# The last norm of a graph network: PE transposes only, DVE adds the residual, and the last sum takes 16 tiles for each group

## The chip, the cores and the metric

The kernel runs on one core of a Trainium2 chip. The metric is device time in microseconds (us) of one execution; lower is better.

## The reference

Four graph layers over 3,125 nodes with 96 features and 100,000 edges, each preceded by a row normalisation and a ReLU and added to the node features. The change touches what lies between the end of the third and the fourth, cut here to:

```python
# end of layer 2 (h comes from its second attention convolution)
h = _graph_norm(h, gn_weight, gn_bias, gn_mean_scale)   # per feature: scale, shift
x = x + _leaky(h + residual, 0.01)
# before layer 3
h = jnp.maximum(_layernorm(x, axis=-1), 0.0)            # per node
# layer 3
norm = deg_inv_sqrt[row] * deg_inv_sqrt[col]
x = x + segment_sum(h[col] * norm[:, None], row)
```

`_leaky(v, s)` is v where v >= 0, else s * v.

## The kernel before

The nodes lie in 25 tiles of 128 rows (NT = 25), taken in 5 groups of 5 tiles (G = 5, NG = 5). The sum over edges is a product with a dense adjacency of 3,200 x 3,200 counts in fp16 (`k.ADJ`), in 25 x 25 blocks of 128 x 128. The summand is split in a high and a low fp16 half (`k.Y`, 192 columns), so a block is one matmul of 128 x 192.

`graph_norm` makes a scale and a shift per feature from column statistics. `last_norm` then runs on all engines at once, each with its own written order and semaphores between them:

- The convolution's output stands turned (features on partitions) in PSUM. ACT, `scaled(g)`, L1964: scale and shift of a group into SBUF (`turned[g]`).
- PE, `raise_rows(g)`: the residual `R` goes through an identity matmul in fp32 into the group's bank (L2008), and five matmuls with an identity turn the scaled tiles back and add them (L2011). `raised(g)` is bank 4 + g % 4.
- Leaky ReLU in two parts, since v + leak = 0.99 relu(v) + 0.01 v. ACT, `bent(g)`, L1971: 0.99 relu of the bank into R. DVE, `bend(g)`, L1897: x + that; `add(g)`, L1901: + 0.01 of the bank.
- DVE, `statistics` (L1909), `moments` (L1914, and the variance, L673), `scales` (L1919 to L1923); ACT, the root (L688), then `rows(g)`: the five tiles normalised with ReLU (L1976) and the high half (L1979). DVE, `low(g)`, L1928: the low half, after which Y of the group is ready.
- PE, L2019: 625 products. `sums(j)` are half banks, tiles 0 to 7 in banks 0 to 3, tiles 8 to 15 in banks 4 to 7, later tiles again from bank 0. `over_chunk(m, first, end)` adds Y's group m to the tiles first to end. Before: groups 0 to 3 for 8 tiles (AT_ONCE = 8), then, after `added` of all groups (the banks of the raise are free), groups 0 to 3 for the next 8, group 4 for all 16, then tiles 16 to 24 one by one.
- DVE, at last, adds the halves (L1954) and the result to x (L1949); SP stores.

ACT's written order is scaled 0 to 3, bent 0, scaled 4, bent 1, bent 2, and for each group the root, bent of g + 3, rows. DVE's order is a loop over g with the six functions staggered. PE first runs 28 matmuls that feed nothing (FILL = 28, L1999).

SP: `load_back` (L1391) loads the residual and the kept x from memory, 5 loads of 240 KB each, in turn (L1394, L1395); behind them on the same queue are the last 6 of 25 transposed loads of the adjacency (L1401), which the products of the last two groups need.

Of the kernel before, what the change touches and what calls it, by code (L numbers as in the profile page):

```python
# [14 lines left out]
ALU = mybir.AluOpType  # L15
ACT = mybir.ActivationFunctionType
# [110 lines left out]
def flat(ap):  # L127
    return ap.rearrange("p a b -> p (a b)")
# [1262 lines left out]
def load_back(k, d, sp):  # L1391

    for g in range(NG):
        sp.dma_start(tiles(k.R, g), tiles(d.residual, g)).then_inc(k.r_back, 16)  # L1394
        sp.dma_start(tiles(k.X, g), tiles(d.kept_x, g)).then_inc(k.x_back, 16)  # L1395


# [467 lines left out]


LEAK = 0.01
FILL = 28


def last_norm(nc, k, d, c, block):

    s = semaphores(nc, k, "last", "scaled raised bent rest added measured row_moments variance deviation row_scale row_factor row_shift "
                   "normal high y_ready unscaled summed emptied final stored")
    R = k.R
    held = flat(k.H[:, :, :])
# [12 lines left out]

    @block.vector
    def _(dve):
        def bend(g):
            dve.wait_ge(s.bent, g + 1)
            dve.wait_ge(k.x_back, 16 * NG)
            dve.tensor_tensor(tiles(k.X, g), tiles(k.X, g), tiles(R, g), ALU.add).then_inc(s.rest, 1)  # L1897

        def add(g):
            dve.wait_ge(s.rest, g + 1)  # L1900
            nc.vector.scalar_tensor_tensor(out=flat(tiles(k.X, g)), in0=raised(g), scalar=LEAK, in1=flat(tiles(k.X, g)),  # L1901
                                           op0=ALU.mult, op1=ALU.add).then_inc(s.added, 1)

        def statistics(g):
            dve.wait_ge(s.added, g + 1)
# [22 lines left out]
            nc.vector.scalar_tensor_tensor(out=part(k.Y, 1, g), in0=tiles(R, g), scalar=SCALE, in1=part(k.Y, 0, g), op0=ALU.mult,  # L1928
                                           op1=ALU.subtract).then_inc(s.y_ready, 1)

        for g in range(NG + 2):
            if g < NG:
                bend(g)
            if 1 <= g <= NG:
                statistics(g - 1)
            if g < NG:
                add(g)
            if 1 <= g <= NG:
                moments(g - 1)
            if g >= 2:  # L1940
                low(g - 2)
            if 1 <= g <= NG:
                scales(g - 1)
        dve.tensor_scalar(k.inv_deg[:, :], k.dis[:, :], 1 / (SCALE * UNIT), None, ALU.mult).then_inc(s.unscaled, 1)
        dve.wait_ge(s.unscaled, 1)

# [13 lines left out]
    @block.scalar  # L1960
    def _(act):
        def scaled(g):
            for t, a, z in turned_spans(g * G, (g + 1) * G):
                last = nc.scalar.activation(turned[g][:, (t - g * G) * P:(t - g * G) * P + z - a], flat(k.ps[0:C, :, :])[:, a:z],  # L1964
                                            ACT.Identity, scale=k.scale, bias=k.shift)
            last.then_inc(s.scaled, 1)

        def bent(g):

            act.wait_ge(s.raised, g + 1)  # L1970
            nc.scalar.activation(flat(tiles(R, g)), raised(g), ACT.Relu, scale=1 - LEAK).then_inc(s.bent, 1)  # L1971

        def rows(g):
            act.wait_ge(s.row_shift, g + 1)
            for t in range(g * G, (g + 1) * G):
                nc.scalar.activation(R[:, t, :], k.X[:, t, :], ACT.Relu, scale=k.row_scale[:, t:t + 1],  # L1976
                                     bias=k.row_shift[:, t:t + 1]).then_inc(s.normal, 1)
            act.wait_ge(s.normal, G * (g + 1))
            nc.scalar.activation(part(k.Y, 0, g), tiles(R, g), ACT.Copy, scale=SCALE).then_inc(s.high, 1)  # L1979

        act.wait_ge(k.affine, 1)
        for g in range(4):
            scaled(g)
        bent(0)
        scaled(4)
        bent(1)
        bent(2)
        for g in range(NG):
            act_row_deviation(nc, k, act, s, g)
            if g + 3 < NG:  # L1990
                bent(g + 3)
            rows(g)

    @block.tensor
    def _(pe):
        def keep_busy(times):

            for _ in range(times):
                nc.tensor.matmul(raised(0)[:, 0:P], k.ident_h[:, :], k.ident_h[:, :], start=True, stop=True)  # L1999

        def raise_rows(g):

            if g >= 4:
                pe.wait_ge(s.added, g - 3)
            elif g >= 1:
                pe.wait_ge(s.scaled, g)
            pe.wait_ge(k.r_back, 16 * NG)
            nc.tensor.matmul(raised(g), k.ident[:, :], flat(tiles(R, g)), start=True, stop=False)  # L2008
            pe.wait_ge(s.scaled, g + 1)
            for t in range(G):  # L2010
                last = nc.tensor.matmul(raised(g)[:, t * C:(t + 1) * C], turned[g][:, t * P:(t + 1) * P], k.ident[0:C, 0:C],  # L2011
                                        start=False, stop=t == G - 1)
            last.then_inc(s.raised, 1)

        def product(j, i):
# [12 lines left out]
                if m == NG - 1 and j % 2:  # L2028
                    last.then_inc(s.summed, 1)

        keep_busy(FILL)
        for g in range(NG):
            raise_rows(g)
        for m in range(NG - 1):
            over_chunk(m, 0, AT_ONCE)
        pe.wait_ge(s.added, NG)
        for m in range(NG - 1):
            over_chunk(m, AT_ONCE, 2 * AT_ONCE)
        over_chunk(NG - 1, 0, 2 * AT_ONCE)
        for j in range(2 * AT_ONCE, NT):  # L2040

            if j % 2 == 0:
# [129 lines left out]
```

## Time and profile before

| | us |
|---|---|
| median of 3 timed executions | 868.24 |
| their lowest and highest | 868.05, 868.81 |
| the profiled execution, all in all | 876.73 |
| its span (all times of the trace run from its start) | 875.0 |
| PE, DVE, ACT busy in it | 750.4, 626.6, 481.2 |
| last stage, from PE's fill to the span's end | 794.3 to 875.0 |

The trace gives for every instruction its start and length; "idle before" is how long its engine had nothing, and what ended that. A PE length includes the way through the array, so lengths of neighbours overlap, and the pace is read from starts. The fp32 matmul has two entries for each instruction. "PEclk" or granted clock is 1.00 at 2.4 GHz and 0.50 at 1.2 GHz.

### The profile page before, as it was taken

The page shows a single profiled execution, that of the slowest core. Times are in us where ns is not written, and L with a number is a line of the kernel's source. Part 1 is how long each engine was busy: PE and PEld are TensorE (multiplying, and loading weights), DVE is VectorE, ACT ScalarE, POOL GpSimd, SP SyncE. Part 2 cuts the span into 40 slices and gives each one's busy share as a digit, 9 for nine tenths or more (in the row PEclk, how much of TensorE's full clock was granted, in tenths as well). Part 3 has the DMA queues.
Part 4 walks back from the last instruction along what each step waited for, and adds up shares of the span by engine and source line. Part 5 has one row for each costly group of instructions (what it writes and reads, how often), then busy time and mean ns, then how long its engine had stood idle before and what let it go on. Part 6 is the DMA issues. An engine that isn't in the chain of part 4 may idle for free. (4 is left out here: it accounts for less than half of the span.)

```text
span 875.0 us, 21046 instructions
## 1 busy us (share of the span) xinstructions
PE 750.4 (86%) x8192; PEld 677.5 (77%) x8192; DVE 626.6 (72%) x1691; ACT 481.2 (55%) x916; POOL 4.3 (0%) x14
## 2 busy tenths in 40 slices
PE   7888888868988999999997399988656999887898
PEld 6655556548987998999997298887655898776797
DVE  7899999985355454433444789998787999885632
ACT  2798889861004222212235578887576988773600
POOL 1000000000000000000000000000000000000000
PEclk9799999998997999999997589999956999996999
DMA  4000000007960000000002100000000699839401
GB/s 135 11 12 12 12 3 1 1 5 262 413 282 1 2 1 2 2 1 1 13 24 81 33 16 4 16 17 1 1 14 20 141 176 200 169 80 233 106 22 36
DMA packets 98739, 56.06 MB, mean 64 GB/s; under 512 B 91160, under 2 KB 93130, under 8 KB 98504
## 3 DMA queue, kind: packets, MB, share of 16 engines
q1 hardware_dynamic: 98292, 53.78, 22.3%
q8 instruction: 69, 1.13, 0.5%
q10 hardware_dynamic: 340, 0.84, 0.3%
q14 instruction: 38, 0.31, 0.1%
HBM read 9.16 MB, written 24.97 MB: 39 GB/s over the span
## 5 line engine op out<-in xcount | busy, mean ns | idle before, releaser
L614 PE MATMUL banks<-y_sb,adjacency 128*128 128x192 f16 (+1 forms) x1875 | 166.4, 249 | 8.5 <-DVE y_sb L651 7.8
L614 PEld LDWEIGHTS banks<-y_sb,adjacency 128*128 128x128 f16 x1875 | 162.0, 99 | 9.5 <-DVE y_sb L651 7.9
L457 PE MATMUL counts<-hot_code,hot_row 128*128 128x100 f16 (+3 forms) x1568 | 122.3, 217 | 23.2 <-DVE hot_code L351 17.6
L457 PEld LDWEIGHTS counts<-hot_code,hot_row 128*128 128x128 f16 x1568 | 90.7, 99 | 66.0 <-DVE hot_code L351 41.3
L1752 PE MATMUL banks<-loose,y_sb 128*128 128x194 f16 x540 | 101.1, 251 | 0.0
L1751 PE MATMUL banks<-x_sb,gat_masks 128*128 128x194 f16 x420 | 79.6, 251 | 20.7 <-DVE gat_masks L1676 6.8
L351 DVE TENSOR_TENSOR hot_code<-codes_iota,unpacked 128x600 f16<-128x600 f16 x196 | 96.7, 552 | 0.0
L560 ACT ACTIVATE adjacency<-counts 128x800 f16<-128x800 f32 x98 | 81.7, 834 | 21.5 <-PE counts L457 21.4
L1751 PE MATMUL banks<-x_sb,y_sb 128*128 128x194 f16 x400 | 75.1, 250 | 13.6 <-DVE h_sb L1676 9.9
L1724 ACT ACTIVATE gat_masks<-y_sb,node_scalars 128x640 bf16<-128x640 f32 x84 | 68.0, 825 | 26.5 <-PE banks L1752 19.3
L1751 PE MATMUL banks<-x_sb,h_sb 128*128 128x194 f16 x430 | 75.8, 247 | 0.8
L1085 ACT ACTIVATE y_sb<-banks 96x256 f32<-96x256 f32 x50 | 19.1, 382 | 97.2 <-PE banks L1117 97.2
L344 DVE TENSOR_TENSOR hot_row<-rows_iota,unpacked 128x2560 f16<-128x2560 f16 x49 | 72.4, 1478 | 0.0
L1752 PE MATMUL banks<-loose,h_sb 128*128 128x194 f16 x400 | 72.4, 247 | 0.0
L1724 ACT ACTIVATE y_sb<-y_sb,node_scalars 128x640 bf16<-128x640 f32 x80 | 64.9, 825 | 10.6 <-PE banks L1752 9.7
L1724 ACT ACTIVATE h_sb<-y_sb,node_scalars 128x640 bf16<-128x640 f32 x86 | 68.2, 825 | 0.4
L640 DVE TENSOR_REDUCE y_sb<-banks 128x96 f32<-128x192 f32 x50 | 17.9, 357 | 65.8 <-PE banks L614 65.8
L539 ACT ACTIVATE distance<-codes_iota,negative 128x100 f16<-128x100 f16 x196 | 57.4, 367 | 11.6 <-DVE negative L336 11.6
L1751 PEld LDWEIGHTS banks<-x_sb,gat_masks 128*128 128x128 f16 x420 | 41.7, 99 | 26.4 <-DVE y_sb L1670 13.1
L640 DVE TENSOR_REDUCE h_sb<-banks 128x96 f32<-128x192 f32 x50 | 17.8, 356 | 59.3 <-PE banks L614 58.8
L1752 PE MATMUL banks<-loose,gat_masks 128*128 128x194 f16 x310 | 58.9, 250 | 0.0
L614 PE MATMUL banks<-loose,adjacency 128*128 128x192 f16 x625 | 55.9, 248 | 0.0
(246 smaller groups left out, 1358.4 us busy)
## 6 DMA issues: line engine op xcount, KB each, us to landing
kept_adj<-adjacency SPq DMA_DIRECT2D x5, 4000.0 KB, 31.8
y_sb<-a_dst_rows SPq DMA_DIRECT2D x10, 320.0 KB, 3.4
window_keys<-edge_keys SPq DMA_DIRECT2D x188, 5.0 KB
residual<-h_sb SPq DMA_DIRECT2D x5, 240.0 KB, 2.0
kept_x<-x_sb SPq DMA_DIRECT2D x1, 1200.0 KB, 4.6
loose<-residual SPq DMA_DIRECT2D x5, 240.0 KB, 4.6
x_sb<-kept_x SPq DMA_DIRECT2D x5, 240.0 KB, 4.8
x_sb<-in_x SPq DMA_DIRECT2D x4, 240.0 KB
```

Source lines behind the costliest of these rows:

```text
L344: dve.tensor_tensor(hot_row[:, h, :, :].rearrange("p n (a b) -> p n a b", b=2), rows_iota[:, :].rearrange("p (a b) -> p a b", b=2).unsquee ...
L351: dve.tensor_tensor(hot_codes(h, b).rearrange("p w (a b) -> p w a b", b=2), codes_iota[:, FROM[b]:FROM[b] + WIDE[b]].rearrange("p (a b) -> ...
L457: last = nc.tensor.matmul(counts[:, 2 * (p % HELD) + i, start:end], hot_row[:, q % 2, b * QUAD + w, :], hot_codes(q % 2, b)[:, w, start - ...
L539: nc.scalar.activation(distance[:, q % 2, w, :], codes_iota[:, FROM[-1]:CODES], ACT.Abs, bias=negative[:, load % 2, at:at + 1]).then_inc(d ...
L560: nc.scalar.activation(k.ADJ[:, :, 2 * p * W:2 * (p + 1) * W].rearrange("p t (b o) -> p t b o", o=W), counts_of(2 * (p % HELD), 2), ACT.Co ...
L614: return nc.tensor.matmul(k.ps[:, j % G, 0:cols], k.ADJ[:, i, j * P:(j + 1) * P], y[:, i, 0:cols], start=i == 0, stop=i == NT - 1)
L640: return nc.vector.tensor_reduce(out, k.ps[:, b, 0:ONE].rearrange("p (q f) -> p f q", q=PARTS), axis=AX, op=ALU.add)
L1085: nc.scalar.activation(HT[:, j % 2, :], k.ps[0:C, TURNED, 0:2 * P], ACT.Copy).then_inc(v.copied, 1)
L1724: nc.scalar.activation(step_of(x), row[ch % 2], ACT.Relu, bias=k.a_s5[:, i:i + 1], scale=STEEP).then_inc(t.step_ready, 1)
L1751: nc.tensor.matmul(bank[:, 0:2 * BC], over_of(x)[:, q * P:(q + 1) * P], features[0][:, i, :], start=i == 0, stop=False)
L1752: return nc.tensor.matmul(bank[:, 2 * BC:4 * BC], under_of(x)[:, q * P:(q + 1) * P], features[1][:, i, :], start=False, stop=i == NT - 1)
```

## The change

- `load_back` issues the five residual loads first and then the five of kept x.
- PE's `raise_rows` only transposes; the identity matmul of R and PE's wait for the residual are gone. The waits on `scaled` stay; for group 4 it waits for the first `lifted`.
- DVE: `lift(g)` adds the residual to the bank, into R; `bend(g)` is max(0.01 R, R) in place; `add(g)` adds it to x. ACT's `bent` is gone.
- DVE's and ACT's written orders are new.
- PE's fill is 32 instead of 28, and a second one of 48 stands behind the raise, into bank 0.
- The sum takes 8 tiles for group 0, waits for all five `lifted`, takes the next 8 for group 0, and then 16 tiles for each of the groups 1 to 4. Tiles 16 to 24 are as before.

```diff
     for g in range(NG):
         sp.dma_start(tiles(k.R, g), tiles(d.residual, g)).then_inc(k.r_back, 16)
+    for g in range(NG):
         sp.dma_start(tiles(k.X, g), tiles(d.kept_x, g)).then_inc(k.x_back, 16)
...
-FILL = 28
+FILL, FILL_MORE = 32, 48
...
+        def lift(g):
+            dve.wait_ge(s.raised, g + 1)
+            dve.wait_ge(k.r_back, 16 * NG)
+            dve.tensor_tensor(flat(tiles(R, g)), raised(g), flat(tiles(R, g)), ALU.add).then_inc(s.lifted, 1)
+
         def bend(g):
+            dve.wait_ge(s.lifted, g + 1)
+            nc.vector.scalar_tensor_tensor(out=tiles(R, g), in0=tiles(R, g), scalar=LEAK, in1=tiles(R, g),
+                                           op0=ALU.mult, op1=ALU.max).then_inc(s.bent, 1)
+
+        def add(g):
             dve.wait_ge(s.bent, g + 1)
             dve.wait_ge(k.x_back, 16 * NG)
-            dve.tensor_tensor(tiles(k.X, g), tiles(k.X, g), tiles(R, g), ALU.add).then_inc(s.rest, 1)
-
-        def add(g):
-            dve.wait_ge(s.rest, g + 1)
-            nc.vector.scalar_tensor_tensor(out=flat(tiles(k.X, g)), in0=raised(g), scalar=LEAK, in1=flat(tiles(k.X, g)),
-                                           op0=ALU.mult, op1=ALU.add).then_inc(s.added, 1)
+            dve.tensor_tensor(tiles(k.X, g), tiles(k.X, g), tiles(R, g), ALU.add).then_inc(s.added, 1)
...
-        for g in range(4):
+        for g in range(NG):
             scaled(g)
-        bent(0)
-        scaled(4)
-        bent(1)
-        bent(2)
         for g in range(NG):
             act_row_deviation(nc, k, act, s, g)
-            if g + 3 < NG:
-                bent(g + 3)
             rows(g)
...
             if g >= 4:
-                pe.wait_ge(s.added, g - 3)
-            elif g >= 1:
-                pe.wait_ge(s.scaled, g)
-            pe.wait_ge(k.r_back, 16 * NG)
-            nc.tensor.matmul(raised(g), k.ident[:, :], flat(tiles(R, g)), start=True, stop=False)
+                pe.wait_ge(s.lifted, g - 3)
             pe.wait_ge(s.scaled, g + 1)
             for t in range(G):
-                last = nc.tensor.matmul(raised(g)[:, t * C:(t + 1) * C], turned[g][:, t * P:(t + 1) * P], k.ident[0:C, 0:C],
-                                        start=False, stop=t == G - 1)
+                last = nc.tensor.transpose(raised(g)[:, t * C:(t + 1) * C], turned[g][:, t * P:(t + 1) * P], k.ident[0:C, 0:C])
             last.then_inc(s.raised, 1)
...
-        keep_busy(FILL)
+        keep_busy(raised(0)[:, 0:P], FILL)
         for g in range(NG):
             raise_rows(g)
-        for m in range(NG - 1):
-            over_chunk(m, 0, AT_ONCE)
-        pe.wait_ge(s.added, NG)
-        for m in range(NG - 1):
-            over_chunk(m, AT_ONCE, 2 * AT_ONCE)
-        over_chunk(NG - 1, 0, 2 * AT_ONCE)
+        keep_busy(sums(0)[:, 0:P], FILL_MORE)
+        over_chunk(0, 0, AT_ONCE)
+        pe.wait_ge(s.lifted, NG)
+        over_chunk(0, AT_ONCE, 2 * AT_ONCE)
+        for m in range(1, NG):
+            over_chunk(m, 0, 2 * AT_ONCE)
```

DVE's written order, where `last_norm` begins. Names of tiles: `loose` holds R, `x_sb` holds x, `banks` is PSUM, `mean` the row deviations. Before:

```order
L1897 TENSOR_TENSOR x_sb<-x_sb,loose 128x480
L1901 SCALAR_TENSOR_TENSOR x_sb<-banks,x_sb 128x480
L1897 TENSOR_TENSOR x_sb<-x_sb,loose 128x480
L1909 BN_STATS y_sb<-x_sb 128x6 x5
L1901 SCALAR_TENSOR_TENSOR x_sb<-banks,x_sb 128x480
L1914 BN_AGGR node_scalars<-y_sb 128x2 x5
L673 TENSOR_SCALAR mean<-node_scalars 128x5
L1919 RECIPROCAL mean<-mean 128x5
```

The same place now:

```order
L1898 TENSOR_TENSOR loose<-banks,loose 128x480
L1902 SCALAR_TENSOR_TENSOR loose<-loose 128x480
L1898 TENSOR_TENSOR loose<-banks,loose 128x480
L1908 TENSOR_TENSOR x_sb<-x_sb,loose 128x480
L1902 SCALAR_TENSOR_TENSOR loose<-loose 128x480
L1915 BN_STATS y_sb<-x_sb 128x6 x5
L1908 TENSOR_TENSOR x_sb<-x_sb,loose 128x480
L1920 BN_AGGR node_scalars<-y_sb 128x2 x5
L673 TENSOR_SCALAR mean<-node_scalars 128x5
L1898 TENSOR_TENSOR loose<-banks,loose 128x480
L1925 RECIPROCAL mean<-mean 128x5
```

Five operations of 128x480 stand before the first statistics instead of three, and a lift of group 2 stands between the first variance and its reciprocal.

DVE further on, from the first scales to the first low half (L1934), now:

```order
L1929 SCALAR_TENSOR_TENSOR node_scalars<-node_scalars 128x5
L1902 SCALAR_TENSOR_TENSOR loose<-loose 128x480
L1915 BN_STATS y_sb<-x_sb 128x6 x5
L1908 TENSOR_TENSOR x_sb<-x_sb,loose 128x480
L1920 BN_AGGR node_scalars<-y_sb 128x2 x5
L673 TENSOR_SCALAR mean<-node_scalars 128x5
L1898 TENSOR_TENSOR loose<-banks,loose 128x480
L1934 SCALAR_TENSOR_TENSOR y_sb<-loose,y_sb 128x5x96
```

Before, the same piece was L1923, L1897, L1909, L1901, L1914, L673, L1928: the bend and the add were there too, and the lift of group 3 is new in it.

PE's written order, from the first fill to the products. Before:

```order
L1999 MATMUL banks<-ident_h 128x128 x28
L2008 MATMUL banks<-loose,ident 128x480
L2011 MATMUL banks<-ident,h_sb 128x96 x5
L2008 MATMUL banks<-loose,ident 128x480
L2011 MATMUL banks<-ident,h_sb 128x96 x5
```

Now:

```order
L1999 MATMUL banks<-ident_h 128x128 x32
L2007 MATMUL banks<-ident,h_sb 128x96 x15
L2007 MATMUL banks<-ident,y_sb 128x96 x10
L1999 MATMUL banks<-ident_h 128x128 x48
L2014 MATMUL banks<-y_sb,adjacency 128x192 x625
```

The matmuls out of `loose` are gone, and the second fill stands directly ahead of the 625 products.

## Rows read from the trace of the kernel before

**Rows 1.** The page of the profile, its first line
```profile
span 875.0 us, 21046 instructions
```

**Rows 2.** The chain that ended last, its last 83 us (start us, length us, engine, tile, line)
```profile
798.08 1.97 PE banks L2008 x2
800.04 2.08 PE banks L2011 x10
...
813.30 0.57 ACT loose L1971
...
816.32 0.66 DVE y_sb L1928
...
828.40 42.34 PE banks L2019 x505
870.76 0.36 DVE h_sb L1954
```

**Rows 3.** PE in order of time in the last stage (start us, length us)
```profile
794.32 3.15 PE L1999 MATMUL banks<-ident_h 128*128 128x128 f16 x28 [2.23 <-PEq L1414]
...
813.10 1.00 PE L2008 MATMUL banks<-loose,ident 128*128 128x480 f32 x2
813.93 1.25 PE L2011 MATMUL banks<-ident,y_sb 96*128 96x96 f32 x10
817.13 3.50 PE L2019 MATMUL banks<-y_sb,adjacency 128*128 128x192 f16 x40 [1.94 <-DVE y_sb L1928]
820.88 3.50 PE L2019 MATMUL banks<-y_sb,adjacency 128*128 128x192 f16 x40 [0.26 <-DVE y_sb L1928]
```

**Rows 4.** Four stretches: PE's busy time, granted clock, DMA share, GB/s
```profile
264.00:270.50 6.50, 5.02 (x25) 0.50 0.00 0
504.30:513.00 8.70, 8.66 (x76) 0.71 0.01 2
792.60:813.00 20.40, 18.07 (x76) 0.50 1.10 254
813.10:817.00 3.90, 2.08 (x14) 1.00 1.12 250
```

**Rows 5.** ACT in order of time, last stage
```profile
796.64 2.67 ACT L1964 ACTIVATE h_sb<-banks,node_scalars 96x640 f32<-96x640 f32 x4 [0.67 <-DVE node_scalars L1857]
...
813.77 1.89 ACT L1976 ACTIVATE loose<-x_sb,node_scalars 128x96 f32<-128x96 f32 x5
815.69 0.60 ACT L1979 ACTIVATE y_sb<-loose 128x480 f16<-128x480 f32 x1
```

**Rows 6.** DVE in order of time, last stage
```profile
802.76 0.66 DVE L1897 TENSOR_TENSOR x_sb<-x_sb,loose 128x480 f32<-128x480 f32 x1 [6.16 <-ACT loose L1971]
803.46 0.66 DVE L1901 SCALAR_TENSOR_TENSOR x_sb<-banks,x_sb 128x480 f32<-128x480 f32 x1
...
810.75 0.17 DVE L1923 SCALAR_TENSOR_TENSOR node_scalars<-node_scalars 128x5 f32<-128x5 f32 x1
810.83 0.66 DVE L1897 TENSOR_TENSOR x_sb<-x_sb,loose 128x480 f32<-128x480 f32 x1
811.40 0.89 DVE L1909 BATCH_NORM_STATS2 y_sb<-x_sb 128x6 f32<-128x96 f32 x5
812.21 0.64 DVE L1901 SCALAR_TENSOR_TENSOR x_sb<-banks,x_sb 128x480 f32<-128x480 f32 x1
812.77 0.43 DVE L1914 BATCH_NORM_AGGREGATE node_scalars<-y_sb 128x2 f32<-128x6 f32 x5
```

**Rows 7.** PE in order of time in an earlier stage: transposes of the same shape
```profile
264.38 2.93 PE L954 MATMUL banks<-ident,loose 96*128 96x96 f32 x15 [3.52 <-ACT loose L910]
...
268.86 1.06 PE L954 MATMUL banks<-ident,loose 96*128 96x96 f32 x5 [0.20 <-ACT loose L910]
```

**Rows 8.** SP's queue in order of time: last load of kept x, transposed loads
```profile
793.15 0.43 SPq L1395 DMA_DIRECT2D x_sb<-kept_x  x1
794.27 22.87 SPq L1401 DMA_TRANSPOSE adjacency<-kept_adj  x6
```

More of the change, by code:

```diff
@@ L1867 @@
 LEAK = 0.01
-FILL = 28
+FILL, FILL_MORE = 32, 48
 def last_norm(nc, k, d, c, block):
-    s = semaphores(nc, k, "last", "scaled raised bent rest added measured row_moments variance deviation row_scale row_factor row_shift "
+    s = semaphores(nc, k, "last", "scaled raised lifted bent added measured row_moments variance deviation row_scale row_factor row_shift "
                    "normal high y_ready unscaled summed emptied final stored")
@@ L1929, in low @@
                                            op1=ALU.subtract).then_inc(s.y_ready, 1)
[L1931 to L1943, printed above, removed]
+        lift(0)
+        bend(0)
+        lift(1)
+        add(0)
+        bend(1)
+        for g in range(NG):
+            statistics(g)
+            if g + 1 < NG:
+                add(g + 1)
+            moments(g)
+            if g + 2 < NG:
+                lift(g + 2)
+            if g >= 1:
+                low(g - 1)
+            scales(g)
+            if g + 2 < NG:
+                bend(g + 2)
+        low(NG - 1)
         dve.tensor_scalar(k.inv_deg[:, :], k.dis[:, :], 1 / (SCALE * UNIT), None, ALU.mult).then_inc(s.unscaled, 1)
@@ L1966, in scaled @@
             last.then_inc(s.scaled, 1)
-        def bent(g):
-            act.wait_ge(s.raised, g + 1)
-            nc.scalar.activation(flat(tiles(R, g)), raised(g), ACT.Relu, scale=1 - LEAK).then_inc(s.bent, 1)
         def rows(g):
@@ L1981, in _ @@
         act.wait_ge(k.affine, 1)
-        for g in range(4):
+        for g in range(NG):
             scaled(g)
-        bent(0)
-        scaled(4)
-        bent(1)
-        bent(2)
         for g in range(NG):
             act_row_deviation(nc, k, act, s, g)
-            if g + 3 < NG:
-                bent(g + 3)
             rows(g)
@@ L1995, in _, with keep_busy @@
     def _(pe):
-        def keep_busy(times):
+        def keep_busy(at, times):
             for _ in range(times):
-                nc.tensor.matmul(raised(0)[:, 0:P], k.ident_h[:, :], k.ident_h[:, :], start=True, stop=True)
+                nc.tensor.matmul(at, k.ident_h[:, :], k.ident_h[:, :], start=True, stop=True)
         def raise_rows(g):
             if g >= 4:
-                pe.wait_ge(s.added, g - 3)
-            elif g >= 1:
-                pe.wait_ge(s.scaled, g)
-            pe.wait_ge(k.r_back, 16 * NG)
-            nc.tensor.matmul(raised(g), k.ident[:, :], flat(tiles(R, g)), start=True, stop=False)
+                pe.wait_ge(s.lifted, g - 3)
             pe.wait_ge(s.scaled, g + 1)
             for t in range(G):
-                last = nc.tensor.matmul(raised(g)[:, t * C:(t + 1) * C], turned[g][:, t * P:(t + 1) * P], k.ident[0:C, 0:C],
-                                        start=False, stop=t == G - 1)
+                last = nc.tensor.transpose(raised(g)[:, t * C:(t + 1) * C], turned[g][:, t * P:(t + 1) * P], k.ident[0:C, 0:C])
             last.then_inc(s.raised, 1)
```

## The prediction

> **What bounds the kernel now.** I begin with the span [rows 1]: 875.0 us. The profiled execution took 876.73 us in all, 1.7 us more than its span; the three timed executions have a median of 868.24 us, 8.5 us less. The sum below is made against the profiled execution and then carried to the median.
>
> Next comes the chain that ended last, over its last 83 us [rows 2]. It runs through PE (from 798.08, when the residual is there: one identity matmul and five half-matmuls for each group of rows, four groups until 813.30), ACT (bend of group 3, then the rows of group 0), DVE (low half of group 0), and then the sum, whose last 505 matmuls run without a gap from 828.40 to 870.74. So the stage has two halves: a run-up that ends when the first group of Y is ready, and 625 matmuls at 42.34 / 505 = 0.0838 us each, 52.4 us that nothing shortens. The question is when the first of them can start and how much PE waits among them.
>
> PE's own order of time [rows 3] answers both. The first product starts at 817.13. The next group's start is 820.88, 3.75 us later, but 40 products take only 3.35 us, so PE waits 0.40 us in each of three gaps, 1.2 us in all. The granted clock [rows 4] is 0.50 (1.2 GHz) from 792.6 to 813.0, while PE was busy for 18.07 of 20.4 us, and 1.00 (2.4 GHz) after that.
>
> ACT [rows 5] shows why the run-up is so long. It is strictly in order: its rows of group 0 start at 813.77, after the bend of group 3 that waited for PE until 813.30. DVE [rows 6] had the row shift of group 0 ready at 810.92. So 2.9 us are lost to ACT's queue, and the rest to PE, which needs 3.8 us a group (15.22 us for four) at the low clock.
>
> **What the change removes.** For each group the identity matmul of 128x480 in fp32 goes (1.7 us: the 3.8 less the 2.08 below) and the half-matmuls, 2.08 us for five [rows 2], become transposes. The same shape, 96x96 in fp32 out of 96x128 weights, is in the trace as transposes at the same 0.50 clock: five in 1.06 us [rows 7], and 15 in 2.93 us, so 0.9 us a group ((2.93 - 1.06) / 2) when they follow one another. ACT loses its five bends, 0.57 us each, and with them its waits for PE. PE no longer waits for the residual.
>
> **The new run-up, step by step.**
> 1. PE fills first: 28 matmuls took 3.15 us from 794.32 [rows 3], 0.1125 us each, so 32 end at 797.92. ACT's first scaled group, at most 0.9 us from 796.64 (three groups, one of them in two pieces, take 2.67 [rows 5]), is done at 797.5 and so hidden. Group 0 is raised at 797.92 + 1.06 = 798.98, group 1 at 799.9, and with 0.9 us a group the last at 802.5. ACT's scaling (0.8 us a group, the last done at about 800.9) hides behind that.
> 2. DVE's lift is an add of 128x480 with one operand in PSUM. There is no such row for this operation; the nearest are 0.66 and 0.64 us for the fused op out of PSUM and 0.66 for the add in SBUF [rows 6]. I take the step between starts: 0.57 us where the next doesn't depend on it (810.83 to 811.40), 0.70 where it does (802.76 to 803.46). The price could be 0.5 to 0.9, which moves the run-up by -0.3 to +1.3 us, as four lifts lie in it.
> 3. Lift 0 at 799.04; bend 0 at 799.74; lift 1 at 800.31; add 0 at 800.88; bend 1 at 801.45; five statistics of group 0 at 802.02 (0.81); add 1 at 802.83; five moments at 803.40 (0.47, 0.43 and the handover); variance at 803.87; lift 2 at 803.97, which hides the root on ACT, as small as DVE's own ops on 5 columns (0.17 us and a handover); three scale ops from 804.54 (0.20 each, 0.17 and the handover). Row shift ready at about 805.1.
> 4. ACT: five rows 1.92 us and the high half 0.60 [rows 5], to 807.7.
> 5. DVE meanwhile: bend 2, statistics 1, add 2, moments 1, variance and lift 3, 0.57 + 0.81 + 0.57 + 0.47 + 0.10 + 0.57 = 3.09 us from 805.03, so low 0 starts at 808.1, not at 807.7: DVE is the last to come. It takes 0.66, and 0.15 us later PE starts, as before. **First product 808.9 instead of 817.13: 8.2 us earlier.**
>
> **What is hidden.** The second fill: 48 matmuls from 802.5 at 0.1125 us are 5.4 us, to 807.9, 1.0 us before Y comes. If the raise were later than I have it, this fill would delay the first product one for one. The loads [rows 8]: the five residual loads are issued first, with no load of kept x between them, and so land before the 798.08 at which PE had them; lift 0 wants them at 799.0. Kept x keeps its last issue at 793.15, and add 0 wants it 7.7 us later. The six transposed loads of the adjacency behind them keep their place on SP's queue; they are issued by 817.1, and the last group's products start at 808.9 + 4 x 6.7 = 835.7. DVE's group costs 4.4 us (0.57 more lift than before, 0.6 of it no longer hidden behind ACT), where the period was 3.75.
>
> **The sum over groups.** With 16 tiles a group PE needs 80 x 0.0838 = 6.7 us for each, more than the 4.4 us in which DVE makes one, so the three waits of 0.40 go. One new wait comes: tiles 8 to 15 use the banks of the raise, and PE waits for the fifth lift. It is behind low 0, the scales, bend 3, statistics 2, add 3 and moments 2 on DVE: 808.1 + 0.57 + 0.6 + 0.57 + 0.81 + 0.57 + 0.57 = 811.8, plus 0.66 = 812.4. PE's first 40 products end at 812.3. A wait of 0.1 to 0.2 us. Net -1.0 us.
>
> From the last products on nothing changes: final tiles at 0.49 us each, the last reduce at 870.76 [rows 2], 4.2 us to the span's end. **Sum: -8.2 - 1.0 = -9.2 us**, 867.5 us for the profiled execution, 859.0 from the median. The terms I could not read (lift, root beside a lift, start-up of the transposes) mostly err to the late side, and a clock that is low for part of the first products costs a little; I take 0.8 us for these and forecast **859.8 us**.
>
> **A rule against the change.** The trace first: 25 transposes in 6.5 us left the clock at 0.50 [rows 4], and PE was busy 5.0 us of it. The identity matmuls that go are, on the other hand, the very work after which it rose at 813. The Trainium skill, TensorE: Matmul & The Clock Gate, Part 4 (PE-mode transpose), says that work in transpose mode does not count as PE being busy, so that the full clock does not come from it. By that rule the raise stays at 1.2 GHz and only the fills can lift the clock; the sum above already has the transposes at their 1.2 GHz price, and the rule bears on rival B.
>
> **Rivals.**
> A. *The profiled execution was unlucky in its clock.* Its stage ran 20 us at half clock, and the timed executions were 8.5 us shorter. At full clock a group took 2.08 us (the last, 813.10 to 815.18 [rows 3]). Had the clock been full from the second group on, group 1 would be raised at 801.9 + 2.1 = 804.0, not 805.7, and group 3 at 808.1. The row shift of group 0 came 5.2 us after the raise of group 1, so it would be there at 809.1, and ACT would start its rows then, 4.7 us sooner than at 813.77. The first product would be at 812.4, and the change would bring 3.5 + 1.0 = 4.5 us: 863.7 us. For: 8.5 us have to be somewhere. Against: the three times lie within 0.76 us of each other, which a clock that rises by chance would not give.
> B. *PE starts the sum at 1.2 GHz.* In an earlier stage fp16 products ran densely from 504.3 on, and the mean clock over the 8.7 us from there is 0.71 [rows 4]: 5 us at 0.50 and 3.7 at 1.00. If the second fill's 5.4 us don't lift it, or it falls in the pause before Y, the first 3.5 to 5.5 us of products run at twice the time, a loss of 1.7 to 2.8 us: 860.7 to 861.8 from the sum's 859.0. For: a clock of 0.50 all through the first fill. Against: the second fill is 5.4 us of fp16 matmuls, and there the clock rose 5 us after such work began, and it did not fall in the pause of 1.94 us before 817.13 [rows 3, 4]. (The skill's rule above speaks for B as well.)
> C. *DVE is slower in the run-up than the sum has it.* It has one more pass over each group. If PSUM reads cost 0.9 us and each handover to a dependent op 0.1 us more, 2 to 3 us of the 9 go: 861 to 862.
> D. *Slower than before.* The clock stays low through the sum's first part as it did through the raise: 20.4 us at 0.50 though PE was busy 18.07 of them. From 808.9 on, each us at 1.2 GHz costs half a us, so the change turns into a loss when the low stretch is over 18.5 us; at 20.4 us it costs 10.2 and gives 869.2 us. Against: the products of 504.3 had the full clock after 5 us.
> E. *The change doesn't do what it says*: PE stalls on the fifth lift for long, because DVE's queue places it behind three groups' work. It would need DVE to be late by more than the 3.35 us of cover; each us late is a us lost. I see 0.1 to 0.2.
>
> **How the numbers follow.** Forecast with its small terms 0.56 (858 to 861), A 0.18 (862 to 865), B 0.14, C 0.08, D 0.03, E 0.01. About 0.2%, 1.7 us, is what a measurement of this kernel can tell from no change, so faster means under 866.5. Only the far end of A, and D, are not: faster 0.93, same 0.03, slower 0.04. The range, 857.3 to 865.0, takes in the sum without allowance and the cheap end of the lift (-0.3), a fill that finds the clock high (1 to 1.4 us), and the whole of B and C and most of A.
>
> **What would show it.** In the profile after: no idle PE before the first transposes, five of them in about 1.06 us at clock 0.50; ACT's rows of group 0 at 10.8 us after PE's first fill begins (805.1 - 794.32; it was 19.5); the first product at 14.6 us after it (808.9 - 794.32; it was 22.8); no idle PE before the second to fifth groups but for the wait on the lift, under 0.3 us; clock 1.00 at the first product. Wrong: a first product over 16 us after the fill begins (C, or the fill itself in its way), the clock at 0.50 there (B, D), or a profile that shows 9 us gained where the times show 5 (A).

## The result and the profile after

| | before | changed |
|---|---|---|
| median of 22 executions each, lowest to highest (us) | 874.0 (868.05 to 878.0) | 868.61 (865.23 to 870.04) |
| profiled execution, its span | 876.73, 875.0 | 869.12, 867.3 |
| PE's first fill begins (in the trace) | 794.32 | 794.89 |
| first product, after the fill's start | 22.81 | 14.22 |
| 625 products, first to last | 53.59 | 53.97 |

The ratio to the kernel before is 0.9946, 95% interval 0.9929 to 0.9964: about 4.7 us faster (3.1 to 6.2), or 5.4 us between the medians. The forecast was 8.4 us. The time itself, 868.61 us, lies above the range that ended at 865.0. Times between kernels are compared below from PE's first fill on, since that point lies at 792.2 to 795.0 us in these traces for reasons ahead of the change, and the place of that point goes into every execution's time.

The page's first line after the change:

```profile
span 867.3 us, 21079 instructions
```

The chain that ended last (start, length, engine, tile, line), which answers [rows 2]:

```profile
794.89 3.57 PE banks L1999 x32
798.46 2.12 PE banks L2007 x15
800.58 0.63 DVE loose L1898
...
804.18 0.66 DVE loose L1898
...
805.82 0.89 DVE y_sb L1915 x5
...
808.40 0.58 DVE y_sb L1934
...
809.11 53.98 PE banks L2014 x625
...
863.12 0.36 DVE h_sb L1965
```

The run-up no longer goes through ACT. From the first raised groups (line 2007) it is DVE all the way to the low half of group 0 (line 1934, 808.40), and the sum is one piece of 625.

PE in order of time, against [rows 3]:

```profile
794.89 3.57 PE L1999 MATMUL banks<-ident_h 128*128 128x128 f16 x32 [2.31 <-PEq L1415]
798.25 2.31 PE L2007 MATMUL banks<-ident,h_sb 96*128 96x96 f32 x15
...
802.01 2.85 PE L1999 MATMUL banks<-ident_h 128*128 128x128 f16 x48
809.11 53.97 PE L2014 MATMUL banks<-y_sb,adjacency 128*128 128x192 f16 x625 [4.25 <-DVE y_sb L1934]
```

Fifteen transposes, three groups, take 2.31 us where the old raise took 3.8 us for each group. The second fill is over at 804.86, PE has nothing for 4.25 us, and the first product comes at 809.11.

The granted clock, against [rows 4] (stretch, length, PE's busy time and count, clock, DMA share, GB/s):

```profile
792.90:799.70 6.80, 4.81 (x42) 0.50 1.10 283
799.90:810.00 10.10, 5.47 (x75) 1.00 1.09 237
810.10:813.40 3.30, 3.30 (x24) 0.50 1.10 248
813.50:817.00 3.50, 3.50 (x44) 1.00 1.36 227
```

The clock rose at 799.8, among the transposes of the raise, was full for all of the second fill, fell at 810.0, 0.9 us after the first product, and was full again at 813.4. So 3.4 us of products ran at half speed, and 53.97 is 1.6 us more than 625 x 0.0838 = 52.4.

ACT and DVE in order of time, against [rows 5, 6]:

```profile
805.37 1.90 ACT L1982 ACTIVATE loose<-x_sb,node_scalars 128x96 f32<-128x96 f32 x5 [0.86 <-DVE node_scalars L1929]
807.30 0.60 ACT L1985 ACTIVATE y_sb<-loose 128x480 f16<-128x480 f32 x1
```

```profile
799.29 0.66 DVE L1898 TENSOR_TENSOR loose<-banks,loose 128x480 f32<-128x480 f32 x1 [2.12 <-PE banks L2007]
799.99 0.66 DVE L1902 SCALAR_TENSOR_TENSOR loose<-loose 128x480 f32<-128x480 f32 x1
800.56 0.65 DVE L1898 TENSOR_TENSOR loose<-banks,loose 128x480 f32<-128x480 f32 x1
...
804.18 0.66 DVE L1898 TENSOR_TENSOR loose<-banks,loose 128x480 f32<-128x480 f32 x1
...
807.74 0.66 DVE L1898 TENSOR_TENSOR loose<-banks,loose 128x480 f32<-128x480 f32 x1
808.32 0.65 DVE L1934 SCALAR_TENSOR_TENSOR y_sb<-loose,y_sb 128x480 f16<-128x480 f32 x1
```

Step by step from the fill's start (794.89), measured and in brackets forecast: lift 0 at 4.40 (4.72), bend 0 at 5.10 (5.42), lift 2 at 9.29 (9.65), ACT's rows at 10.48 (10.8), low 0 at 13.43 (13.8), first product 14.22 (14.6). The lift takes 0.66 us, or 0.57 to the next start, like the operation in SBUF. The new run-up is what the prediction said, 0.3 to 0.4 us early throughout. The clock isn't the reason: lift 0 started at 799.29, before the clock rose, and was already 0.32 us early. The sum let the first transposes start when the fill was over, 3.60 us after it began; they started 3.36 us after it (798.25), as the records of neighbours overlap. The faster transposes after that gained nothing, since lift 1 came 0.57 us after bend 0, at DVE's own pace.

### The profile page after: what moved, and what is told of

Its sections match the earlier page's. It is cut to its first block and busy times, and to the rows that moved or that the text cites. A ratio compares the mean times of both kernels' runs of the same rounds, so it can differ in the third digit from the quotient of the medians.

```text
span 867.3 us, 21079 instructions
## 1 busy us (share of the span) xinstructions
PE 740.7 (85%) x8209; PEld 670.8 (77%) x8209; DVE 629.3 (73%) x1696; ACT 478.6 (55%) x911; POOL 4.3 (0%) x14
## 3 DMA queue, kind: packets, MB, share of 16 engines
q1 hardware_dynamic: 98292, 53.78, 22.8%
## 5 line engine op out<-in xcount | busy, mean ns | idle before, releaser
L2014 PE MATMUL banks<-y_sb,adjacency 128*128 128x192 f16 x625 | 54.0, 250 | 4.3 <-DVE y_sb L1934 4.3
```

Source lines behind the costliest of these rows:

```text
L2014: return nc.tensor.matmul(sums(j), k.ADJ[:, a * G + i % G, at:at + P], k.Y[:, i, 0:ONE], start=i == 0 and j % 2 == 0, stop=i == NT - 1 and ...
```

## Experiments

Four sets were run, each on one chip together with the kernel before, whose median in the set stands beside (870.88, 875.59, 874.79, 874.65). The last two columns are from the one trace that each has.

| run | median us (n) | before in its set | ratio, 95% interval | first product after fill | products |
|---|---|---|---|---|---|
| changed, again | 867.61 (12) | 870.88 | 0.9942, 0.9919 to 0.9965 | 14.22 | 53.97 |
| old order of products | 867.62 (12) | 870.88 | 0.9953, 0.9928 to 0.9978 | 14.23 | 53.97 |
| bridge, 80 fills | 865.73 (7) | 870.88 | 0.9924, 0.9894 to 0.9954 | 14.22 | 52.48 |
| no second fill | 868.96 (12) | 870.88 | 0.9956, 0.9930 to 0.9982 | 14.22 | 54.44 |
| before, again | 875.14 (12) | 875.59 | 1.0011, 0.9977 to 1.0045 | 16.10 | 53.60 |
| before, new order alone | 876.87 (12) | 875.59 | 1.0023, 0.9989 to 1.0056 | 22.96 | 56.70 |
| before, first fill of 60 | 871.03 (12) | 875.59 | 0.9971, 0.9942 to 0.9999 | 17.46 | 53.97 |
| short chain, 80 fills | 865.82 (10) | 875.59 | 0.9909, 0.9879 to 0.9939 | 13.98 | 52.34 |
| short chain, 36 fills | 866.55 (7) | 874.79 | 0.9917, 0.9889 to 0.9946 | 12.84 | 54.84 |
| own chain, 36 fills | 868.89 (12) | 874.79 | 0.9942, 0.9921 to 0.9963 | 14.22 | 54.44 |
| loads in turn | 868.39 (12) | 874.79 | 0.9938, 0.9917 to 0.9959 | 14.22 | 53.97 |
| short chain, 42 fills | 866.26 (6) | 874.65 | 0.9905, 0.9880 to 0.9931 | 12.85 | 52.34 |

The ratio compares all executions of a set and isn't the quotient of the two medians, which swing with the kernel before: its median alone lies anywhere from 870.9 to 875.6 us.

### The kernel before, once more: where its time goes up and down

No edit.

> The kernel before as it is, for more of its own executions with their clocks and one more trace. Theory 1 (the clock in the raise is what makes it vary): executions from 868 to 878 us; where PE's clock rises in the raise, a group takes about 2.1 instead of 3.7 us and the first product comes up to 4.7 us sooner after PE's first fill than the 22.8 us of the trace known so far. Theory 2: the first product is always 22.8 us after the fill, and the variation comes from elsewhere in the program.

Its profiled execution took 870.26 us, and its trace differs from the first one in the raise. PE in order of time:

```profile
794.53 3.15 PE L1999 MATMUL banks<-ident_h 128*128 128x128 f16 x28 [2.08 <-PEq L1414]
798.15 1.76 PE L2008 MATMUL banks<-loose,ident 128*128 128x480 f32 x2 [0.47 <-DMA loose<-residual]
799.75 1.25 PE L2011 MATMUL banks<-ident,h_sb 96*128 96x96 f32 x10
800.83 1.00 PE L2008 MATMUL banks<-loose,ident 128*128 128x480 f32 x2
...
807.44 1.25 PE L2011 MATMUL banks<-ident,y_sb 96*128 96x96 f32 x10
810.63 3.50 PE L2019 MATMUL banks<-y_sb,adjacency 128*128 128x192 f16 x40 [1.94 <-DVE y_sb L1928]
```

The clock in the same trace (the same columns as above):

```profile
792.80:799.50 6.70, 4.50 (x30) 0.50 1.08 283
799.70:810.60 10.90, 8.99 (x59) 1.00 1.11 243
```

And ACT, where its rows of group 0 start:

```profile
807.27 1.89 ACT L1976 ACTIVATE loose<-x_sb,node_scalars 128x96 f32<-128x96 f32 x5
```

Here the clock was full from 799.6 on, a group of the old raise took 1.93 us (798.15 + 2.7 for the first, then 800.83, 802.76), ACT began its rows of group 0 at 807.27 and not at 813.77, and the first product came at 810.63, 16.1 us after the fill began and not 22.8. The span is 868.5 us, 6.5 us shorter than in the first trace; the stage makes 6.7 of it. The 132 executions of the kernel before in all sets fall in two heaps: 47 from 867 to 872 us and 85 from 872 to 880, with 76 of these between 874 and 878. The two traces, 870.26 and 876.73 us, stand one in each. That every execution of the lower heap has the early clock is inferred, not seen in each, but two numbers on record agree with it. Of the 110 executions in the four sets, whose mean granted clock is known, it is 0.933 or more in 21 of the 37 below 872 us and in none of the 73 above. And the heaps have means of 869.5 and 875.6 us, 6.1 us apart, where the stage differs by 6.7. What makes the clock rise early in one execution and late in another was not found. The first three timed executions, on which the prediction stood, were all of the lower heap.

### Only a longer first fill in the kernel before

```diff
-FILL = 28
+FILL = 60
```

> The kernel before with a first fill of 60 matmuls instead of 28. Theory 1: the clock is full at the start of the raise; it starts about 2.3 us later (800.3 for 798.0) but takes 2.1 us a group, so the first product comes 3.5 to 4.5 us sooner than in the known trace, the median falls by 2 to 4 us, and the executions lie within 3 us of each other. Theory 2: the raise starts later and gains nothing, 0 to 3 us slower.

PE in order of time in this kernel, and a stretch of its granted clock:

```profile
794.64 5.88 PE L1999 MATMUL banks<-ident_h 128*128 128x128 f16 x60 [2.17 <-PEq L1414]
...
812.10 53.97 PE L2019 MATMUL banks<-y_sb,adjacency 128*128 128x192 f16 x625 [1.94 <-DVE y_sb L1928]
```

```profile
812.10:816.60 4.50, 4.50 (x36) 0.63 1.22 213
```

The fill took 5.9 us, the clock was full from 799.7, the raise ran at 1.92 us a group, and the first product came 17.46 us after the fill began: 5.3 us sooner than in the first trace, though PE started its raise 2.0 us later after that point. Eleven of twelve executions lie between 869.16 and 872.37 us (one outlier of 1821 us aside), so the upper heap is gone. The median fell by 4.6 us against 875.59 in the set; by the ratio, 0.9971, it is 2.5 us, and the interval, 0.9942 to 0.9999, is wide, since the kernel beside it varies. The clock fell here too, at 813.3, 1.2 us after the first product, and cost the products 1.6 us (53.97). One number in the old kernel thus gave about half of what the whole change gave: 2.5 us of 4.7 by the two ratios, whose intervals overlap. The changed kernel lies 2.2 us lower by the ratios and 3.0 us by the means of its 34 executions and these eleven (867.99 and 870.97); in the traces the two differ by 3.2 us in this stage (17.46 - 14.22).

### The new order of products alone

In the kernel before, PE's `over_chunk` calls replaced by those of the changed kernel, with `added` for `lifted`:

```diff
-        for m in range(NG - 1):
-            over_chunk(m, 0, AT_ONCE)
+        over_chunk(0, 0, AT_ONCE)
         pe.wait_ge(s.added, NG)
-        for m in range(NG - 1):
-            over_chunk(m, AT_ONCE, 2 * AT_ONCE)
-        over_chunk(NG - 1, 0, 2 * AT_ONCE)
+        over_chunk(0, AT_ONCE, 2 * AT_ONCE)
+        for m in range(1, NG):
+            over_chunk(m, 0, 2 * AT_ONCE)
```

> The kernel before with only the new order of products (8 tiles of group 0, a wait for the last add, the next 8, then 16 tiles for each later group). The fifth add of the old run-up ends 6.0 us after the first product starts, 2.7 us after the first 40 products: PE waits 2.7 us once instead of 1.2 us in three gaps. So this part alone should cost 1.5 us; a gain of 1 us would mean that the order is good by itself.

PE waited 2.60 us for the fifth add, as expected, and the products took 56.70 us, 3.1 more than before, where 1.5 were expected: the clock fell as well, at 823.2 when PE resumed, and was low for 3.4 us, which costs another 1.7. Against its neighbours the median is 1.3 to 1.7 us higher; the ratio's interval, 0.9989 to 1.0056, doesn't exclude no change. In the old run-up the new order brings nothing, and no run shows it bringing anything in the new one (below).

### The changed kernel again, and with the old order of products

> The changed kernel as it is, as the measure for its neighbours. Theory 1 (clock): the second fill ends early when the clock is already full, PE then idles some 4 us before the first product, the clock falls, and the first 3 to 4 us of products run at 1.2 GHz: 625 products take about 54.0 us from the first to the last, 1.6 more than at full clock. Theory 2 (run-up or chance): nothing systematic in the clock; a new execution shows the products in 52.4 us. Against the kernel before, 4 to 7 us less by either.

> The changed kernel with the old order of the products (8 tiles for groups 0 to 3, the next 8 tiles afterwards). PE then waits for DVE before groups 1 to 3: starts of the groups 4.13, 3.76 and 3.76 us apart where 40 products take 3.35, 1.6 us of waiting. If my sum is right (the 16 tiles a group bring 1.0 us at full clock) this is 1.0 to 1.4 us slower than the changed kernel. If the clock is low at the first product (theory 1), the slow products fall into those waits, and the difference is 0 to 0.5 us. If 16 tiles a group were the main part of the gain, it would be 3 us or more.

```diff
-        over_chunk(0, 0, AT_ONCE)
-        pe.wait_ge(s.lifted, NG)
-        over_chunk(0, AT_ONCE, 2 * AT_ONCE)
-        for m in range(1, NG):
-            over_chunk(m, 0, 2 * AT_ONCE)
+        for m in range(NG - 1):
+            over_chunk(m, 0, AT_ONCE)
+        pe.wait_ge(s.lifted, NG)
+        for m in range(NG - 1):
+            over_chunk(m, AT_ONCE, 2 * AT_ONCE)
+        over_chunk(NG - 1, 0, 2 * AT_ONCE)
```

The changed kernel repeats to 0.01 us: 14.22 and 53.97. With the old order nothing changes, 867.62 against 867.61 us and again 53.97 us: the 625 products follow one another without a gap in both. At half clock the first of them take longer, which gives DVE the time. The 1.0 us that the prediction gave to this part does not show. What the new order would bring at full clock was not tried.

### The clock at the first product: more fill, none, and where it stands

```diff
-        keep_busy(sums(0)[:, 0:P], FILL_MORE)
+        keep_busy(sums(0)[:, 0:P], 24)
+        pe.wait_ge(s.row_moments, G)
+        keep_busy(sums(0)[:, 0:P], 24)
+        pe.wait_ge(s.row_shift, 1)
+        keep_busy(sums(0)[:, 0:P], 24)
+        pe.wait_ge(s.high, 1)
+        keep_busy(sums(0)[:, 0:P], 8)
```

> The changed kernel with the second fill of 48 matmuls cut in four and spread over the wait for Y: 24 after the raise, 24 after the moments of group 0, 24 after its row shift, 8 after its high half. Theory 1: the clock is full at the first product, the 625 products take 52.4 to 52.6 us, and the kernel is 1.3 to 1.7 us faster than the changed one. Theory 2: no difference (within 0.3 us).

PE in order of time in the kernel with the bridge, from the second fill on:

```profile
799.42 1.50 PE L1999 MATMUL banks<-ident_h 128*128 128x128 f16 x24
801.54 2.85 PE L1999 MATMUL banks<-ident_h 128*128 128x128 f16 x48 [0.62 <-DVE node_scalars L1920]
805.37 0.62 PE L1999 MATMUL banks<-ident_h 128*128 128x128 f16 x8 [0.98 <-ACT y_sb L1985]
806.52 52.48 PE L2014 MATMUL banks<-y_sb,adjacency 128*128 128x192 f16 x625 [0.53 <-DVE y_sb L1934]
```

Its granted clock:

```profile
797.30:806.50 9.20, 6.72 (x96) 1.00 1.13 251
806.50:812.00 5.50, 5.48 (x64) 1.00 1.13 205
```

With PE kept at work until Y is there the clock stays at 1.00 and the products take 52.48 us, 1.49 less. The first product is where it was, 14.22 us after the fill. The median is 1.9 us below the changed kernel's in the same set; all seven executions are under 866.7, though the intervals of the two ratios overlap. Theory 1 stands by the traces.

No second fill at all:

```diff
-FILL, FILL_MORE = 32, 48
+FILL, FILL_MORE = 32, 0
```

> The changed kernel without the second fill. Theory 1: PE idles from the raise to the first product, 6 to 7 us, so the clock is always low there and comes 3.4 to 6 us later: 54.0 to 55.2 us for the products, 0 to 1.2 us slower than the changed kernel, as the fill of 48 already loses most of its purpose. Theory 2: no difference.

PE in order of time in this kernel, and then its granted clock:

```profile
807.60 54.44 PE L2014 MATMUL banks<-y_sb,adjacency 128*128 128x192 f16 x625 [6.93 <-DVE y_sb L1934]
```

```profile
798.50:801.70 3.20, 1.80 (x16) 1.00 1.10 249
801.90:811.90 10.00, 4.30 (x28) 0.50 1.09 235
812.10:816.00 3.90, 3.90 (x49) 1.00 1.11 240
```

PE idles for 6.93 us, the clock is low from 801.8 and full again from 812.0, 4.4 us into the sum, and the products take 54.44 us, 0.47 more than with the fill of 48. The median is 1.35 us higher than the changed kernel's, of which the stage shows 0.47. By the products, the second fill as written gives 0.47 of the 1.96 us (54.44 - 52.48) that one which bridges the pause gives.

The spread fill again, with 36 in place of 80:

```diff
-        keep_busy(sums(0)[:, 0:P], FILL_MORE)
+        keep_busy(sums(0)[:, 0:P], 14)
+        pe.wait_ge(s.row_moments, G)
+        keep_busy(sums(0)[:, 0:P], 10)
+        pe.wait_ge(s.row_shift, 1)
+        keep_busy(sums(0)[:, 0:P], 8)
+        pe.wait_ge(s.high, 1)
+        keep_busy(sums(0)[:, 0:P], 4)
```

> The changed kernel with its own order on DVE and the spread fill of 36 matmuls instead of one fill of 48 (14 after the raise, 10 after the moments, 8 after the row shift, 4 after the high half). If it is the place of the fill and not its amount that keeps the clock, the products take 52.4 to 52.6 us and this is as fast as the bridge of 80, 1.3 to 1.9 us faster than the changed kernel, with 12 matmuls less. If the amount counts, the clock falls before the first product as in the changed kernel: 53.9 us or more for the products, no gain.

Its granted clock:

```profile
798.80:805.40 6.60, 3.93 (x48) 1.00 1.09 246
805.60:812.20 6.60, 4.91 (x32) 0.50 1.07 238
```

This guess failed: the clock fell at 805.5 and the products took 54.44 us, as with no second fill. With the waits at the same places, 80 held the clock and these 36 did not. Whether it is the number or the way it is shared out can't be told from this: below, 42 held it, but with the portions changed as well.

### A shorter chain for group 0 on DVE

The bridge of 80, and in DVE's written order what group 0 needs moved ahead of the work for later groups:

```diff
+        statistics(0)
+        moments(0)
+        lift(2)
+        scales(0)
         bend(1)
-        for g in range(NG):
-            statistics(g)
-            if g + 1 < NG:
-                add(g + 1)
-            moments(g)
-            if g + 2 < NG:
-                lift(g + 2)
-            if g >= 1:
-                low(g - 1)
-            scales(g)
-            if g + 2 < NG:
-                bend(g + 2)
-        low(NG - 1)
+        lift(3)
+        add(1)
+        statistics(1)
+        low(0)
+        moments(1)
+        lift(4)
+        scales(1)
...
+        scales(4)
+        low(4)
```

> The changed kernel with the second fill spread over the wait (as in the run with the bridge) and a shorter way for group 0 on DVE: the bend and add of group 1 no longer stand ahead of the statistics and moments of group 0, and low 0 stands ahead of the moments of group 1. Theory (DVE's written order sets the first product, not PE or ACT): first product 12.9 us after PE's first fill begins instead of 14.2, and the kernel 1.2 to 1.5 us faster than the bridge alone, 3.0 to 3.4 faster than the changed kernel. Rival: lifts or the second group come late and PE waits; then the gain is under 0.5 us.

PE and then DVE in order of time in this kernel (the second fill is here at line 2016, the products at 2031):

```profile
799.75 6.64 PE L2016 MATMUL banks<-ident_h 128*128 128x128 f16 x80
806.22 18.94 PE L2031 MATMUL banks<-y_sb,adjacency 128*128 128x192 f16 x225
```

```profile
803.79 0.66 DVE L1934 SCALAR_TENSOR_TENSOR y_sb<-loose,y_sb 128x480 f16<-128x480 f32 x1
```

The chain worked: low 0 was done at 804.45, 12.2 us after the fill began. But in this execution the clock stood otherwise than in the other traces. It was full in the first fill and low from 797.1 on:

```profile
797.20:803.80 6.60, 6.52 (x53) 0.50 1.11 240
```

So the 80 fills took 6.6 us, and PE came to the first product 1.8 us after Y was ready. A fill that is hidden at 2.4 GHz was not at 1.2. The expected 1.2 to 1.5 us over the bridge are 1.3 by the ratios, with intervals that overlap, and nothing by the medians (865.82 and 865.73). The same chain with the fills of 14, 10, 8 and 4 in place of 24, 24, 24 and 8:

```diff
-        keep_busy(sums(0)[:, 0:P], 24)
+        keep_busy(sums(0)[:, 0:P], 14)
...
```

> The short chain on DVE again, but the spread fill is cut from 80 to 36 matmuls (14, 10, 8, 4), 3.9 us at 1.2 GHz, which fit between the raise and Y even if the clock is low. In the run with 80 the clock was low and the fill ended 1.8 us after Y of group 0 was ready. Theory (that fill hid the gain of the short chain): first product 12.4 to 12.9 us after PE's first fill begins, and 1.0 to 1.8 us faster than with 80. Rival (the gain of the short chain is lost to something else, as late lifts): within 0.5 us of it.

Its granted clock at the first product (807.87):

```profile
806.40:813.00 6.60, 5.74 (x37) 0.50 1.06 230
```

First product at 12.84, as expected, but the clock fell 1.6 us before it (at 806.3) and the products took 54.84 us: the 1.4 us won ahead were more than half lost behind (54.84 - 53.97 = 0.9). This traced execution, 868.76 us, is the slowest of its seven; the median is 866.55. "1.0 us faster than with 80" did not come: by the medians of two sets it is 0.7 us slower, by the ratios 0.7 too (0.0008 x 875), with intervals that overlap.

The fill between the two, 42, with its weight moved to the longer waits:

```diff
-        keep_busy(sums(0)[:, 0:P], 14)
+        keep_busy(sums(0)[:, 0:P], 10)
         pe.wait_ge(s.row_moments, G)
         keep_busy(sums(0)[:, 0:P], 10)
         pe.wait_ge(s.row_shift, 1)
-        keep_busy(sums(0)[:, 0:P], 8)
+        keep_busy(sums(0)[:, 0:P], 14)
         pe.wait_ge(s.high, 1)
-        keep_busy(sums(0)[:, 0:P], 4)
+        keep_busy(sums(0)[:, 0:P], 8)
```

> The short chain on DVE with a spread fill of 42 matmuls, 10, 10, 14 and 8, so that more of them stand between the row shift and the high half, where the fill of 36 left PE idle for 2 us. Theory (the short chain is worth 1.4 us and the kept clock 1.5 us, and both can be had at once): first product 12.8 us after PE's first fill begins, the 625 products in 52.4 to 52.6 us, no low clock at the first product; 2.5 to 3.3 us faster than the changed kernel, ratio to the kernel before 0.989 to 0.991. Rival: the clock falls before the first product again, as with 36; then the products take 53.5 to 54.5 us and the ratio is 0.991 to 0.993.

PE in order of time in this kernel:

```profile
800.10 0.72 PE L2016 MATMUL banks<-ident_h 128*128 128x128 f16 x10
801.21 0.73 PE L2016 MATMUL banks<-ident_h 128*128 128x128 f16 x10 [0.39 <-DVE node_scalars L1920]
802.48 0.96 PE L2016 MATMUL banks<-ident_h 128*128 128x128 f16 x14 [0.53 <-DVE node_scalars L1929]
805.05 0.62 PE L2016 MATMUL banks<-ident_h 128*128 128x128 f16 x8 [1.61 <-ACT y_sb L2002]
805.83 52.34 PE L2031 MATMUL banks<-y_sb,adjacency 128*128 128x192 f16 x625 [0.16 <-DVE y_sb L1934]
```

Its granted clock up to the first product:

```profile
797.90:805.80 7.90, 4.86 (x59) 1.00 1.09 244
```

Both at once in this trace: 12.85 us to the first product and 52.34 us for the products, which is the floor of 625 x 0.0838. The profiled execution took 864.18 us, against 868.85 and 869.12 for the changed kernel; 1.6 and 1.9 us of that lie ahead of the stage, since its fill began at 792.98 and theirs at 794.61 and 794.89. The median of its six executions is 866.26 and the ratio 0.9905 (0.9880 to 0.9931), against 0.9942 and 0.9946 for the changed kernel, so about 3 us faster; but by their times it can't be told from the bridge (0.9924) or the short chain with 80 fills (0.9909), whose intervals overlap it. Its traced execution is at the lower end of 863.81 to 867.28 us; whether the others lose their time ahead of this stage or to a clock that stands otherwise in them was not settled.

### The order of the loads

```diff
     for g in range(NG):
         sp.dma_start(tiles(k.R, g), tiles(d.residual, g)).then_inc(k.r_back, 16)
-    for g in range(NG):
         sp.dma_start(tiles(k.X, g), tiles(d.kept_x, g)).then_inc(k.x_back, 16)
```

> The changed kernel with the residual and kept x loaded in turn, as before. The residual then lands about 3.7 us after PE's first fill begins, and the first lift needs it at 4.4 us: my prediction holds the order of the loads to be hidden, so no difference to the changed kernel (within 0.4 us). Rival: the lift waits for it, 0.5 to 1.5 us slower.

The first product came at 14.22 and the products took 53.97 us, and the ratio is 0.9938 against 0.9942. The order of the loads is hidden, as the prediction had it.

## Why the prediction was right and wrong

- **The run-up** (-8.2 us, first product at 14.6 after the fill) was right for the trace it was read from: 14.22, so -8.6. DVE as the last to come, the lift's price (0.57) and the hidden loads hold. No run takes the identity matmuls or ACT's bends out alone, so how the gain is shared between them stays open.
- **The step that failed first: carrying the sum to the median.** The text took 868.24 us as the kernel before and -9.2 us as the gain, but the two belong to different clocks of PE in the raise. 868.24 lies in the heap whose one trace has an early clock, and from there the run-up has only 16.1 - 14.2 = 1.9 us to win; the gain was read from a trace with a late one, where it is 8.6. Over 22 executions before has its median at 874.0. Of the 8.8 us between 868.61 and the forecast of 859.8, 5.8 are this baseline and 3.0 the gain (5.4 for 8.4). Rival A named this mechanism, with the first product 4.7 us sooner (measured 6.7) and 863.7 us, and gave it 0.18; the three times within 0.76 us, held against it, were three draws from one heap. If executions fall into the heaps independently, that has a chance of 0.05 ((47 / 132) cubed), so it was bad luck, or neighbours in time are alike; no run tells which. Rival A was also priced against the wrong end: what varies is mostly before's time, not the changed kernel's (868.6, spread 4.8 us against 10).
- **The term that was mis-sized: the sum over groups**, -1.0 us. Measured +0.4 (53.97 against 53.59), because the clock was low at the first products: the three waits did go, 1.2 us, and 1.6 us of low clock came. That the stage's whole gain in the two first traces, 8.2 us (8.6 - 0.4), is so near to the net forecast of 8.4 is luck: the run-up gave 0.4 more, the sum 1.4 less, and 0.8 had been set aside. The two orders of products give the same 53.97.
- **What was taken as hidden: the second fill.** It was costed as 48 matmuls at 1.2 GHz, 5.4 us that end 1.0 us before Y. The clock rose in the raise, so it ended after 2.85 us and left PE idle for 4.25. Rival B had the loss about right (1.7 to 2.8 us; 1.6 and, in other runs, 2.0 and 2.5), and of its two reasons the second came near: the fill did not fail to lift the clock, it was over too soon to hold it through the pause, which the run with the bridge shows. B was given 0.14; the pause of 1.94 us held against it was less than half of the 4.25 us that came.
- **The rule of the Trainium skill** (TensorE: Matmul & The Clock Gate, Part 4: PE-mode transpose: transpose mode does not count as PE being busy in the same way, and the full clock doesn't engage for it) did not forecast what the raise did here, and is neither shown nor refuted. In the changed kernel's trace PE did nothing but transposes from 798.46 and the clock rose at 799.8, in the middle of them, so the raise did not stay at 1.2 GHz. In the kernel before, with fp32 matmuls in their place, it rose at 799.6 in one trace and at 813.0 in another. The matmuls of the fill came before, so the trace doesn't prove that transposes alone would raise it. In the run with no second fill the clock was full from 798.4, PE did nothing but transposes, and it fell at 801.8, which the rule would fit.
- C, D and E did not occur: DVE was 0.3 to 0.4 us early, no low clock held for more than 5 us into the sum, and the wait for the fifth lift did not appear.

With the clock of before as it falls, an expectation can now be put together, after the fact, from the heaps: 85 of 132 executions win 8.2 us in the stage (22.8 + 53.6 - 14.2 - 54.0), 47 win 1.5 (16.1 + 53.6 - 14.2 - 54.0): 5.8 us in the mean, beside the measured 4.7 (3.1 to 6.2). The heaps bear it out one by one: the changed kernel's 34 executions have a mean of 868.0 us, 7.6 us below the upper heap's 875.6 and 1.5 below the lower one's 869.5.

## What to carry to other kernels

A trace shows one execution; before a gain read from it is subtracted from a median, ask whether the resource that makes the gain (here PE's clock in the stage) is the same in the executions behind that median, and take the spread of many as part of the baseline. Work that only keeps the clock up has two lengths, one at each clock: it must reach to the next real work at the fast one and still end in time at the slow one, so it is better cut up and tied to the progress of what is waited for. And if a stage's time hangs on the clock, try the fill's length first: one constant in the old kernel gave about half of what the rewrite gave.

## What the runs showed of the hardware that was not expected

- The same code gave a clock that was full 5.1 us after the fill began (794.53 to 799.6) in one execution and 18.7 us after it (794.32 to 813.0) in another, with PE at work nearly all the time between, mostly on fp32 matmuls.
- The clock can fall after a pause, with PE at work again: in the changed kernel PE idled for 4.25 us, resumed at 809.11, and the clock went down at 810.0, with products running, and came back at 813.4. After a pause of 1.94 us it held in both traces of the kernel before and fell at 813.3, 1.2 us into the products, in the one with a fill of 60.
- DVE's add of 128x480 with an operand in PSUM took 0.66 us and 0.57 to the next start (800.56 to 801.13), the same as with both in SBUF.
